# One core, a convolution and attention kernel: input areas in DRAM, a merged bias load, and a different split and order of the value and denominator sums

## The reference

```python
x_norm = group_norm(x, gn1_gamma, gn1_beta, 32).reshape(b, c, n)         # n = 256, c = 128
q, k, v = split(einsum('oc,bcn->bon', qkv_w, x_norm) + qkv_b)            # 8 heads of 16
attn = softmax(einsum('bhnd,bhmd->bhnm', q, k) / sqrt(16))
x_attn = einsum('bhnm,bhmd->bhnd', attn, v)                              # values / denominators
x_attn = group_norm(einsum('oc,bcn->bon', out_w, x_attn) + out_b, gn2_gamma, gn2_beta, 32)
h1, gate = split(x_attn @ mlp1_w.T)                                      # 512 each
return x + (silu(h1) * gate) @ mlp2_w.T
```

## Time and profile before

| what | us |
|---|---|
| median of 3 runs | 148.97 |
| lowest and highest of them | 148.63, 149.8 |
| the profiled execution | 148.53 |
| its span in the profile | 146.7 |

### The profile page before, as it was taken

One profiled execution on the slowest core, in us unless ns is written; L12 is line 12 of the kernel. 1 busy time (PEld: TensorE's weight loads), 2 busy tenths in 40 slices (PEclk: granted clock), 3 DMA queues, 4 the chain that ended last, 5 costly groups with the idle time before them and its releaser, 6 DMA issues.

```text
span 146.7 us, 3222 instructions
## 1 busy us (share of the span) xinstructions
PE 139.9 (95%) x1140; PEld 124.0 (84%) x1140; DVE 81.9 (56%) x171; ACT 94.9 (65%) x213; POOL 68.9 (47%) x134
## 2 busy tenths in 40 slices
PE   6959998999999998999999999999999999999992
PEld 5839988998999787798799699699699699799981
DVE  1733133157648778788779558746497351343441
ACT  6835798996248886797586774459377396934220
POOL 6005889983003877140792223870223874634500
DMA  3789800752520160522503404301001000101111
GB/s 83 202 273 374 280 2 14 200 150 68 153 69 0 30 190 3 143 74 69 152 2 109 114 2 137 118 0 36 7 0 36 2 7 0 36 4 36 38 36 36
DMA packets 12368, 12.05 MB, mean 82 GB/s; under 512 B 1728, under 2 KB 11328, under 8 KB 12352
## 3 DMA queue, kind: packets, MB, share of 16 engines
q1 hardware_dynamic: 12208, 11.81, 27.2%
q10 hardware_dynamic: 144, 0.04, 0.1%
HBM read 4.44 MB, written 1.05 MB: 37 GB/s over the span
## 4 chain that ended last, share of the span: by engine, by line
PE 77%; SPq 9%; DMA 5%; issue 2%; DVE 2%; POOL 2%; POOLq 0%
PE pm L815 10%; PE po L866 10%; PE ps L841 10%; PE px L942 9%; SPq L279 6%; PE pf L725 4%; PE pf L727 4%; PE pf L726 4%; DMA wqk_s<-in_wqk 3%; PE pf L775 2%; PE pf L743 2%; PE po L775 2%; PE po L890 2%; DMA k_stack<-qk_parts 2%; PE px L797 2%
## 5 line engine op out<-in xcount | busy, mean ns | idle before, releaser
L1494 DVE TENSOR_REDUCE neg_max<-pm 128x2 f32<-128x512 f32 x64 | 41.9, 686 | 11.9 <-PE pm L815 11.5
L515 ACT ACTIVATE up_t<-ps 128x512 f32<-128x512 f32 x64 | 35.4, 594 | 12.5 <-PE po L866 8.0
L815 PE MATMUL pm<-k_stack,q_stack 127*128 127x256 f32 x128 | 26.5, 304 | 0.7 <-DMA k_stack<-qk_parts 0.6
L841 PE MATMUL ps<-q_stack,k_stack 128*128 128x256 f32 x128 | 26.2, 299 | 0.0
L815 PEld LDWEIGHTS pm<-k_stack,q_stack 127*128 127x128 f32 x128 | 19.1, 189 | 2.6 <-issue 1.2
L841 PEld LDWEIGHTS ps<-q_stack,k_stack 128*128 128x128 f32 x128 | 19.4, 190 | 1.0 <-ACT up_t L515 0.4
L866 PE MATMUL po<-up_t,v_aug 128*32 128x256 f32 x256 | 15.7, 382 | 0.2 <-DVE gs L1451 0.2
L942 PE MATMUL px<-win,w_s 128*128 128x256 f32 x56 | 15.3, 389 | 0.0
L725 PE MATMUL pf<-xm_hi,w_hi 128*128 128x256 f32 x44 | 13.5, 307 | 0.0
L404 POOL TENSOR_SCALAR masked<-sums,vec 128x256 f32<-128x256 f32 x8 | 3.8, 481 | 18.8 <-ACT sums L533 18.8
L727 PE MATMUL pf<-xm_hi,w_lo 128*128 128x256 f32 x44 | 12.3, 280 | 0.0
(11 more groups left out here) (135 smaller groups left out, 318.0 us busy)
## 6 DMA issues: line engine op xcount, KB each, us to landing
q_stack<-qk_parts SPq DMA_DIRECT2D x24, 128.0 KB, 2.4
k_stack<-qk_parts SPq DMA_DIRECT2D x24, 128.0 KB, 2.4
win<-in_xw SPq DMA_DIRECT2D x12, 128.0 KB, 5.3
win<-in_xw SPq DMA_DIRECT2D x6, 256.0 KB, 6.0
out<-win SPq DMA_DIRECT2D x8, 128.0 KB, 1.7
w_s<-in_w SPq DMA_DIRECT2D x1, 512.0 KB, 4.6
w_s<-in_w SPq DMA_DIRECT2D x1, 256.0 KB, 5.3
wqk_s<-in_wqk SPq DMA_DIRECT2D x1, 128.0 KB, 4.7
```

The lines of the kernel that those rows point to most:

```text
L515: act.activation(probs[:, h // HALF, h % HALF, :, :].rearrange("p c n -> p (c n)"), ps[:, h % 2, :], ACT.Exp, scale=D ** -0.5).then_inc(pr ...
L815: return pe.matmul(pm[:, h % 2, c * N:(c + 1) * N], stack_rows(q_stack, i, slice(0, TOP))[:, h, c * 128:(c + 1) * 128], stack_rows(k_stack ...
L841: return pe.matmul(ps[:, h % 2, c * N:(c + 1) * N], stack_rows(k_stack, i, slice(0, TOP + 1))[:, h, c * 128:(c + 1) * 128], stack_rows(q_s ...
L1494: dve.tensor_reduce(neg_max[:, i % 2, 2 * h:2 * h + 2], pm[:, h % 2, :].rearrange("p (c n) -> p c n", c=2), AX.X, ALU.max, negate=True).th ...
```

## The change

1. The first half of x (images 0 to 3) is stored as `xw[2, 256, 256]`, so that the rows of one piece follow one another without a gap; images 4 to 7 as `xh[256, 512]`. The host prepares both.
2. The bias stands as 128 more columns in `factors`, so that one DMA issued by ScalarE brings both, and the bias DMA at the head of SP's list goes. A new constant `swap` (64 KB) is loaded ahead of `wqk`.
3. The warm-up is three products of 256 columns and one of 128 in place of five of 256.
4. `merge` leaves POOL. ACT reads columns 0 to 255 of `po` twice, each time times one mask of rows (`early`), and DVE adds columns 256 to 511 times the other mask: one addition gives `dens` with all denominators, one `merged` with all values. `turn_sums` turns `dens` in two pieces (not four); what it multiplies by is `swap_s`, an identity whose blocks of 16 are exchanged in pairs, so that the heads come out in order. It now waits for both additions, as it overwrites `po`.
5. The orders of all engines are new.

```diff
-WARM_UP = 5
+WARM_UP = [N, N, N, N // 2]
...
-            sp.dma_start(bias_bc[:, :], bass.AP(tensor=bias0.tensor, offset=0, ap=[[0, 128], [1, C]])).then_inc(bias_in, 16)
...
-                    sp.dma_start(win_at(t, q, n), xw[r0:r0 + 128, q * Q:(q + n) * Q]).then_inc(win_in[t][q], 16)
+                    sp.dma_start(win_at(t, q, n), xw[q, r0:r0 + 128, :] if n == 1 else xh[r0:r0 + 128, :]).then_inc(win_in[t][q], 16)
...
+            sp.dma_start(swap_s[:, :], swap).then_inc(w_in, 16)
...
-            def merge(i):
-                pool.wait_ge(sums_ready, i + 1)
-                if i:
-                    pool.wait_ge(weighted_ready, i)
-                pool.tensor_scalar(masked[:, 0, :], sums[:, 0, :], half_rows[0], 0.0, ALU.mult, ALU.add).then_inc(masked_made, 1)
-                pool.tensor_scalar(masked[:, 1, :], sums[:, 1, :], half_rows[1], 0.0, ALU.mult, ALU.add).then_inc(masked_made, 1)
-                pool.wait_ge(masked_made, 2 * (i + 1))
-                pool.tensor_tensor(merged[:, :], masked[:, 0, :], masked[:, 1, :], ALU.add).then_inc(merged_ready, 1)
...
             def read_sums(i):
                 act.wait_ge(pv_done, 2 * (i + 1))
                 if i:
-                    act.wait_ge(weighted_ready, i)
-                act.activation(sums[:, :, :].rearrange("p a n -> p (a n)"), po[:, 0, :], ACT.Copy).then_inc(sums_ready, 1)
+                    act.wait_ge(merged_ready, i)
+                act.activation(early[:, 1, :], po[:, 0, 0:N], ACT.Copy, scale=half_rows[1]).then_inc(early_ready, 1)
+                act.activation(early[:, 0, :], po[:, 0, 0:N], ACT.Copy, scale=half_rows[0]).then_inc(early_ready, 1)
...
             def turn_sums(i):
-                pe.wait_ge(sums_ready, i + 1)
+                pe.wait_ge(dens_ready, i + 1)
+                pe.wait_ge(merged_ready, i + 1)
                 for c in range(2):
-                    for half in range(2):
-                        a = (2 * c + half) * 128
-                        mm = pe.transpose(po[:, 0, a:a + 128], sums[:, half, c * 128:(c + 1) * 128], ident_s[:, :])
+                    mm = pe.transpose(po[:, 0, c * 128:(c + 1) * 128], dens[:, c * 128:(c + 1) * 128], swap_s[:, :])
                 mm.then_inc(den_done, 1)
...
+            def merge(i):
+                dve.wait_ge(pv_done, 2 * (i + 1))
+                dve.wait_ge(early_ready, 2 * (i + 1))
+                if i:
+                    dve.wait_ge(den_done, i)
+                dve.scalar_tensor_tensor(out=dens[:, :], in0=po[:, 0, N:2 * N], scalar=half_rows[0], in1=early[:, 1, :],
+                                         op0=ALU.mult, op1=ALU.add).then_inc(dens_ready, 1)
+                if i:
+                    dve.wait_ge(weighted_ready, i)
+                dve.scalar_tensor_tensor(out=merged[:, :], in0=po[:, 0, N:2 * N], scalar=half_rows[1], in1=early[:, 0, :],
+                                         op0=ALU.mult, op1=ALU.add).then_inc(merged_ready, 1)
...
# one place of ACT's new order
             read_y(2)
+            fill(2, 0)
             high_parts(0)
-            fill(2, 0)
             read_y(3)
+            fill(2, 1)
             read_early_v(0)
```

More of the change, by code:

```diff
@@ L77, with build @@
 GN1 = len(GN1_BATCHES)
-def build(nc, xw, factors, bias0, vecs, wqk, wv, wo, w1, w2,
-          ident, gmat, out):
+def build(nc, xw, xh, factors, vecs, wqk, wv, wo, w1, w2,
+          ident, gmat, swap, out):
     ctx = ExitStack()
@@ L981, in _ @@
             upsample(14)
-            project_qk(2)
             maxima(0, 4, 0)
+            upsample(15)
             maxima(0, 4, 1)
@@ L986, in _ @@
             maxima(0, 5, 1)
-            upsample(15)
+            project_qk(2)
+            downsample(5)
             maxima(0, 6, 0)
@@ L1145, in _ @@
             scores(3, 2, 1)
+            scores(3, 3, 0)
+            scores(3, 3, 1)
             project_v(6)
-            turn_sums(2)
             maxima(5, 0, 0)
             maxima(5, 0, 1)
-            turn_maxima(4)
-            scores(3, 3, 0)
-            scores(3, 3, 1)
             scores(3, 4, 0)
             scores(3, 4, 1)
-            project_qk(7)
+            turn_sums(2)
+            scores(3, 5, 0)
+            scores(3, 5, 1)
+            up_project(0, 0, 0)
+            turn_maxima(4)
+            scores(3, 6, 0)
+            scores(3, 6, 1)
+            turn_inverse(2)
+            up_project(0, 0, 1)
+            scores(3, 7, 0)
+            scores(3, 7, 1)
             maxima(5, 1, 0)
+            project_out(2)
             maxima(5, 1, 1)
@@ L1317, in _ @@
             maxima(7, 7, 1)
+            scores(6, 4, 0)
+            scores(6, 4, 1)
+            up_project(5, 0, 0)
+            scores(6, 5, 0)
+            scores(6, 5, 1)
+            turn_inverse(5)
+            up_project(5, 0, 1)
+            scores(6, 6, 0)
+            scores(6, 6, 1)
+            up_project(5, 1, 0)
+            project_out(5)
+            up_project(5, 1, 1)
             scores(6, 7, 0)
+            scores(6, 7, 1)
+            turn_maxima(7)
+            down_project(3, 0)
             up_project(6, 0, 0)
             up_project(6, 0, 1)
-            up_project(6, 1, 0)
-            scores(6, 7, 1)
-            up_project(6, 1, 1)
-            turn_maxima(7)
+            group_means(5)
+            down_project(3, 1)
             weigh(6, 0, 0)
@@ L1328, in _ @@
             weigh(6, 1, 1)
-            down_project(6, 0)
-            down_project(6, 1)
-            turn_sums(6)
-            up_project(7, 0, 0)
             scores(7, 0, 0)
@@ L1616, in _ @@
             reduce_max(6, 3)
             reduce_max(6, 4)
+            read_means(4)
             swish_value(2)
             reduce_max(6, 5)
-            residual(0)
             gate(2)
             reduce_max(6, 6)
+            reduce_max(6, 7)
+            merge(4)
+            reduce_max(7, 0)
+            invert(4)
+            normalise(4)
+            for j in range(1, 4):
+                reduce_max(7, j)
             swish_value(3)
-            invert(4)
+            reduce_max(7, 4)
@@ L1662, in _ @@
             residual(5)
-            gate(13)
+            for j in range(13, 16):
+                gate(j)
             residual(6)
-            gate(14)
-            gate(15)
             residual(7)
```

652 lines of the change are left out of this document (312 added, 340 removed).

## The result

The changed kernel takes 147.75 us (median of 4 runs, 146.87 to 148.52), the kernel before 149.38 (median of 4). The ratio is 0.9897, with a 95% interval of 0.985 to 0.9944: 1.0% faster, where the forecast had 1.9%. The time lies in the range, the gain is about half of what was forecast. A few executions are slow, some by hundreds of us; medians and ratios are of the others alone.

The account below looks back on a forecast made before the run. TensorE was taken as the bound. From the profiled 148.53 us, -1.76 - 0.9 - 0.3 - 0.2 + 0.4 = -2.76 gave 145.8, or 146.2 after the 0.4 offset to the median; 8-in-10 range 144.0 to 148.6.

Parts of the forecast that it names:

- What bounds the kernel: From some 23 to 144.18 us, nearly every microsecond of TensorE work removed should come out of the time.
- Fewer turned columns: In turn_sums, two of four products go for each of 8 images: 16 x 0.11 = 1.76 us won, all counted.
- The start: Up to the first maxima: earlier, evenly landing windows, partly given back later; 0.9 us won, between 0.5 lost and 2.4 won.
- The clock: Rival, chance 0.05: after the shorter warm-up the first 12 upsample records run at 0.43 us, not 0.22; 148.2 us.
- The stack wait: TensorE's 0.8 us wait for image 3's stack DMA: 0.3 us won, bounds 0.8 won and 0.7 lost.
- the end: Wait of 0.3 us ahead of the last down_project: two more products before the gate's use win 0.2 us.
- The new chain of the sums: From weigh to turn_sums, 1.2 us longer but mostly covered by other work: 0.4 us lost, bounds 0 and 9.6.
- VectorE as the bound: Rival, chance 0.08: VectorE's additions ahead of the maxima make it set the pace of images 0 to 5; 151.0 us.
- The merge chain eats the turn's gain: Rival, chance 0.15: turn_sums or turn_inverse waits 0.3 us per image, 2.4 us in place of 0.4; 148.2 us.
- the clean start: Rival, chance 0.15: the start comes out clean and the new order fills all waits, -5.3 us; 143.8, centre 144.2.

Follow-up runs that it names:

- the start alone: Kernel before with only the contiguous DRAM layout of x and the bias beside the factors: 147.48 us (0.9894), repeated at 148.0 (0.9937).
- run with the long warm-up: Changed kernel with five warm-up products of 256 columns, as before: 148.01 us, 0.9927 of the kernel before.
- run with the small products: Changed kernel plus 14 unused 32 x 4 products ahead of the group means of images 2 and 3: 147.81 us, 0.9901 of the kernel before.
- turn of maxima first: Changed kernel with turn_maxima(1) ahead of weigh(0, 0) and ScalarE reading the row one exponential earlier: 147.27 us, 0.9883 of the kernel before.
- the areas alone: Kernel before with only x stored in contiguous DRAM areas, the bias keeping its own DMA: 148.15 us, 0.9953 of the kernel before.
- the changed kernel with the old areas: Changed kernel with x stored as before, rows of a piece 4 KB apart: 149.77 us, 1.0048 of the kernel before.
- the run with the new sums alone: Kernel before with merge on VectorE, early on ScalarE and two turned pieces, merge one step ahead of each reciprocal: 157.32 us, 1.0533.

## Why the prediction was wrong about the size

**What bounds the kernel: right.** TensorE is still 95% of the span, and its share of the chain rose from 77% to 87%.

**Fewer turned columns, -1.76: the work right, its worth too large.** 16 products are gone, and giving them back cost 1.55 us of body and 1.0 us of the median. I had counted all of them as standing between other products.

**The start, -0.9: the sign right, the size too small.** The maxima start 1.61 us earlier; in the medians the start alone is worth 0.0063 to 0.0106 of 149, so 0.9 to 1.6 us (two runs). The median time of a window piece fell from 5.3 to 3.2 us, and the wait for the sixth window went, as said:

```profile
win<-in_xw SPq DMA_DIRECT2D x12, 128.0 KB, 3.2
```

I had taken a middle value because I expected ScalarE's fills and `project_qk(0)` to take much of it back. They took less: the wait ahead of `project_qk(0)` became one of 1.0 us ahead of the group means, 0.4 us more than before.

**The clock: the rival's event came, its price did not.** The first eight upsample records took 3.08 us and the next eight 1.89, so 1.2 us were lost, nearly what the start at 4.32 and not 5.59 had won. But it is not there in each execution. In the third trace of the changed kernel the same records ran at full speed:

```profile
4.31 1.94 PE L722 MATMUL ps<-win,up_w 128*128 128x256 f32 x8
```

and its maxima start only 0.3 us earlier (28.85). The run with the long warm-up is as fast. The Trainium skill (TensorE: Matmul & The Clock Gate, Part 1: The HAM clock gate) says that sustained activity, not a number of products, releases the clock. The traces agree: the one program ran 13, 15 and 8 records at 1.2 GHz in its three traces.

**The stack wait, -0.3, and the end, -0.2.** The first went entirely (0.8 us) in this execution, though in the run with the small products 0.7 us of it are back. The second did not: 0.4 us where it was 0.3.

**The new chain of the sums, +0.4: this is the step that failed.** "The new list does put more scores and up-projections between", I wrote, and asked only whether each `turn_sums` comes late enough. It does: there is no wait for `dens` or `merged` in the changed kernel, and its length was well estimated, as two rows show (mean in ns behind the comma):

```profile
L1479 DVE SCALAR_TENSOR_TENSOR dens<-po,vec,early 128x256 f32<-128x256 f32 x8 | 3.9, 483 | 5.1 <-ACT early L512 2.6 <-PE po L845 1.2 <-issue 1.2
L1483 DVE SCALAR_TENSOR_TENSOR merged<-po,vec,early 128x256 f32<-128x256 f32 x8 | 3.8, 475 | 0.0
```

What I put at nothing is what the order paid for that cover. `weigh(0, 0)` went ahead of `turn_maxima(1)`, which gives the sums an earlier start, and the row of image 1 was issued just ahead of a transfer of instructions and came late: TensorE waited 1.1 to 1.5 us for it in the three traces. I had looked at the order around image 2 only, not at the row's path, and took a small DMA's landing for constant. The sum by the runs: from the first mark on, -1.76 was forecast for the columns and -0.3 - 0.2 + 0.4 = -0.1 for the rest, so -1.9; measured +0.8. Of the 2.7 us between, the row is 0.7 to 1.15 (turn of maxima first; 0.6 in the medians). For the rest I counted TensorE's records, each at the spacing that its kind shows back to back, and took the sum from the time: from 42 to 66 us, 2.5 to 3.2 us are without a product before, 4.9 to 5.3 in the changed kernel, 4.2 to 4.6 with the turn of the maxima first, by how the spacing is taken. (The busy column hides most of this, since the ends of matmuls are modelled.) So by this estimate 1.4 to 1.7 us more than before are lost in that stretch even with the row in time, in pauses of which none is over 0.5 us; two of them are the waits of 0.2 us or so ahead of `turn_inverse`, for `inv_wide`, and ahead of `project_v`, for VectorE:

```profile
54.07 0.44 PE L863 MATMUL po<-ident_s,inv_wide 128*128 128x128 f32 x2 [0.22 <-ACT inv_wide L519]
...
54.77 0.68 PE L776 MATMUL px<-wv_s,win 128*128 128x128 f32 x4 [0.26 <-DVE qk_parts L1454]
```

These rows are of the changed kernel. None of these pauses was tested singly, so their causes stay open; shown is where they lie.

**VectorE as the bound: rightly given little.** It is busy for 9.66 of 10 us from 60 to 70 and TensorE for 9.91 in the same stretch. The reserve was smaller than by my 9.3, but no wait of TensorE for VectorE over 0.4 us stands in this kernel behind the start.

**The rivals.** "The merge chain eats the turn's gain" (148.2) is, with the clock's 148.2, nearest in time, and wrong in its mechanism: no 0.3 us per image, but one wait for a DMA and a few pauses. In the old order, though, its mechanism is there in full, with 8 us. Two slips in the prediction change nothing: the clean start's sum gives 143.7, not 143.8, and the new warm-up is 8 records, the last two of half the length, not 7.

## What to carry to other kernels

Work taken off the bounding engine is worth its price only if the order that makes it possible leaves the other waits covered; read the new order at each short chain with a DMA in it (here turn, read, 8 KB copy, scores), not only at the chain that was changed. Undo or do the parts of a large change singly: here the smallest part, where the input lies in DRAM and who loads the bias, was the whole gain, and a large rewrite of sums and orders was worth nothing until one block of products was put back (147.27, 0.7 us under the start alone in the same series). Give a small DMA on the path more than its usual time: its usual 1.8 us became 3.0 to 3.7 at one place of the new order, in nine of nine traces (seven kernels).

## What the runs showed of the hardware that I had not expected

- An 8 KB DMA spread over 16 engines usually lands in 1.8 us; at one place of the new order it took 3.0 to 3.7 in nine of nine traces, because one of its 16 parts was 1.2 to 2.0 us behind. In these nine and in four more (image 6 in the old order, 2.7 to 3.1 us), a transfer of instructions of 16 KB and about 1 us began 0.7 to 1.6 us behind the issue, and the late packet ended 0.04 to 0.07 us behind its end. One that began later or at the issue cost little: at 1.81 us behind it (the kernel with the turn first) the row took 1.9, at 0 to 0.15 us behind it 2.0 to 2.6. That the late packet stood in line behind the instructions is what these times suggest; the records don't name the engine of each packet, and the run meant to part the two did not move the transfer enough.
- Rows of 1 KB that lie 4 KB apart in DRAM take longer to land than the same rows without gaps: 5.3 us in the median before and 3.4 with the areas alone, 4.7 in the changed kernel with the old areas and 3.2 with the new. Before, the sixth piece landed 3.05 us behind the fifth, with the areas alone 0.35. It is worth 0.5% of the kernel before by itself.
- TensorE's granted clock reads 1.00 in the stretch from 0 to 6 us, while warm-up and first upsample records run at half rate: the column does not show this state at the start, the spacing of equal records does. A fall in mid-run it does show (0.55 from 10.5 to 14 us in the run with the new sums alone).
